# Walking the edges of two attention hops in batches of four steps

## Chip, cores and metric

The kernel runs on one core of one Trainium2 chip. The metric is the device time of one execution in microseconds (us). The kernel before takes 5588.73 us, the median of 3 runs (5587.19 to 5595.54).

## What is computed

A chain of four graph layers on 3125 nodes of 64 features and 100,000 edges (src, dst, a type of 32), each followed by a residual and a layer norm: a GIN layer, an attention layer with two hops, a GAT layer with a GRU gate, and four Chebyshev convolutions. The change is in the second layer, whose one hop is

```python
def _agg(entity_emb, relation_emb, W, head, tail, edge_type):
    a_input = jnp.concatenate([entity_emb[head], entity_emb[tail]], axis=-1)
    e = jnp.sum(a_input @ W * relation_emb[edge_type], axis=-1)
    e = jax.nn.leaky_relu(e, LEAKY_SLOPE)
    m = jax.ops.segment_max(e, head, num_segments=n)
    ex = jnp.exp(e - m[head])
    denom = jax.ops.segment_sum(ex, head, num_segments=n)
    alpha = ex / denom[head]
    return jax.ops.segment_sum(entity_emb[tail] * alpha[:, None], head, num_segments=n) + entity_emb
```

head is src and tail is dst. Per edge: a score, a maximum over all edges of the same head, and a sum weighted by the exponential of the gap to that maximum.

## The kernel before

The edges are sorted by head. 128 edges make a tile (782 of them, NT), four tiles a group (196, NG), 128 nodes a block (25, NB). A walk of BSTEPS = 196 + 25 - 1 = 220 steps goes through pairs (group, block): each step handles the four tiles of one group against one block of heads, and then either the group or the block advances. Which pair a step has is known only at run time; it is in `S.walk` and is loaded into registers with `load_row`, eight steps at a time. The walk is done once per hop, by `hop_edges`, fully unrolled.

In a step, five engines work in a pipeline with lags written out by hand in `lagged(...)`; each engine executes its stages in that order, and each stage waits on semaphores for its inputs and for buffers to come free:

- GpSimd (`on_pool`) fetches a row of 97 numbers of `dram_table` for each edge of the group (the features of the tail, a one, and its 32 scores by type), with one indirect DMA for each tile, into `ring`, which holds RG = 40 groups. It runs ahead as far as the ring allows (L969: it waits for the sum of step g - 40 + 24) and with at most 8 groups not landed.
- VectorE makes `hot` (L1102, edge against head, 0 where the edge's head is that lane) and `typed` (L1101). TensorE turns `hot` (L995), ScalarE copies the turned one to `hot_t` and counts in hop 0 (L1037). TensorE adds the tails' scores and the heads' scores, looked up by `hot_t`, in a bank (L1013, L1017).
- VectorE picks the type and sums (L1109, L1120, L1131), ScalarE spreads the score to `reach` [edge, head] with a far value where the edge isn't of that head (L1046, four instructions a step). VectorE takes the maximum over the four tiles (L1115, L1126), folds it with a running maximum kept for each block and lane, `most` (L1139, L1147); TensorE turns it (L1007), VectorE reduces it to the largest per head (L1078). ScalarE makes the factor `fade` by which older sums shrink, and keeps `held` (L1058, L1060).
- TensorE spreads the largest to all rows (L1001), VectorE subtracts (L1082), ScalarE takes the exponential (L1063), TensorE sums the rows of the ring by those weights (L983), VectorE adds the sum to the accumulator (L1092).

During the layer the first HELD = 6 of 25 blocks of the arena `adjacency` stay, and the other 19 are in `dram_adjacency`; they are written out ahead of the GIN layer (L2164) and read back after the second hop (L1272), and `gat_attention` waits for them (L1346).

Of the kernel before, what the change touches and what calls it, by code (L numbers as in the profile page):

```python
# [8 lines left out]
ALU = mybir.AluOpType  # L9
# [19 lines left out]
AHEAD = 8  # L29
# [7 lines left out]
HELD = 6  # L37
RG = 40
WRING = 8
# [897 lines left out]
def hop_edges(k, carve, cst, psum, dram, S, ring, own_parts, acc, hop):  # L937
# [3 lines left out]

    W1 = D + 1
    most = carve("most", [P, NB, P], F32)
    held = carve("held_largest", [P, NB], F32)
    hot = carve("other_source", [P, 6, P, TG], BF16)
    hot_t = carve("own_source", [P, 3, TG * P], BF16)
    reach = carve("in_reach", [P, WRING, TG, P], F32)
    typed = carve("type_hot", [P, 4, TG, NREL], BF16)
    picked = carve("picked", [P, 2, TG, NREL], F32)
    raw, score = carve("raw_score", [P, 2, TG], F32), carve("score", [P, 2, TG], F32)  # L950
    pairs, lane = carve("lane_pairs", [P, 2, 2, P], F32), carve("lane", [P, 2, P], F32)
    now, fade = carve("largest_now", [P, 4], F32), carve("fade", [P, 4], F32)
    tiles = [min(TG, NT - g * TG) for g in range(NG)]
    tails = [k.sig(f"tails{r}", 16) for r in range(8)]
    step_cols, hot_made, turned, own_made = k.sig("step_columns"), k.sig("own_hot"), k.sig("own_turned"), k.sig("own_copied")
    looked, picks, raws, scored, reached = k.sig("own_looked"), k.sig("type_picked"), k.sig("raw_made"), k.sig("step_scored"), k.sig("step_reached")
    paired, laned, most_made, lane_turned = k.sig("lanes_paired"), k.sig("lane_made"), k.sig("step_most"), k.sig("lane_turned")
    largest, spread, faded, held_made = k.sig("largest_made"), k.sig("largest_spread"), k.sig("fade_made"), k.sig("largest_held")
    kept, gaps, weighed, summed, added, counts = k.sig("most_kept"), k.sig("sum_gap"), k.sig("sum_weights"), k.sig("block_summed"), k.sig("block_added"), k.sig("degree_added")
    landed = lambda g: tails[g % 8].at(sum(tiles[g % 8:g + 1:8]) - 1)  # L960
    row = lambda t, at: t[:, bass.ds(at, 1), :].rearrange("p o c -> p (o c)")
    scores, lookups, lanes, rows, sums = psum[0:2], psum[2:4], psum[4], psum[5], psum[6:8]
# [11 lines left out]

    def on_pe(pe):
        at_j, at_r = {}, {}
        for stage, i in lagged(BSTEPS, (8, 0, 6, 5, 1)):
            if stage == 0:
                pe.wait_ge(weighed.sem, weighed.at(i))
                if i >= 2:  # L980
                    pe.wait_ge(added.sem, added.at(i - 2))
# [1230 lines left out]
```

## Time and profile before

| | us |
|---|---|
| median of 3 runs | 5588.73 |
| profiled execution | 5621.36 (span 5620.0) |
| walk of hop 1, first gather to last addition | 1341.2 to 2767.6 |
| walk of hop 2 | 2819.9 to 4235.9 |

| engine | busy us | share of the span |
|---|---|---|
| TensorE matmul | 3745.6 | 67% |
| VectorE | 3241.2 | 58% |
| ScalarE | 2395.8 | 43% |
| GpSimd | 1999.8 | 36% |

No engine is busy all the time, so the shares say little. The two walks together are half of the execution, and the change touches them, a short set-up ahead of them and the transfer of `dram_adjacency` behind them. The views to read are the busy time in stretches of a walk, and the instructions of each engine in order of time within one. A wait called "remote" is one for a semaphore whose releaser the profile doesn't show as just finished; "issue" is time in which the engine waited for nothing that the profile shows.

### The profile page before, as it was taken

What the parts mean: (1) busy time and instruction counts of PE and PEld (TensorE: products, weight loads), DVE (VectorE), ACT (ScalarE), POOL (GpSimd) and SP (SyncE); (2) the same over time, 40 slices, a digit from 0 to 9 for tenths busy, and PEclk for the clock granted to TensorE, in tenths of its full rate; (3) what the DMA queues carried; (4) which work ended last, traced back from release to release, by engine and by line L of the source; (5) the groups of instructions that cost most, each with busy time, mean ns of one, the idle gap of its engine ahead of it and who ended that gap; (6) DMA issues with size and microseconds to landing.
All of it is one profiled execution on the core that took longest, in us unless ns stands there. A gap on an engine that the chain in (4) does not pass through costs nothing. (4 is left out here: it accounts for less than half of the span.)

```text
span 5620.0 us, 85456 instructions
## 1 busy us (share of the span) xinstructions
PE 3745.6 (67%) x22845; PEld 2857.0 (51%) x22846; DVE 3241.2 (58%) x10029; ACT 2395.8 (43%) x6908; POOL 1999.8 (36%) x2011
## 2 busy tenths in 40 slices
PE   3388888692076666667803776776793188778987
PEld 0144444381076666666703766666682077654443
DVE  8888888523065555556703654554574888744444
ACT  0255555431064454445602544444462755523321
POOL 5000000333716666664073466666610065401210
PEclk6699999795555555555555555555555555578997
DMA  0000000201101111111020011111102000000000
GB/s 9 6 0 0 0 0 0 113 2 27 39 7 33 33 33 33 34 33 25 5 42 21 23 34 34 33 34 33 33 7 112 0 1 1 2 9 4 4 2 12
DMA packets 72030, 122.19 MB, mean 22 GB/s; under 512 B 40834, under 2 KB 45867, under 8 KB 71147
## 3 DMA queue, kind: packets, MB, share of 16 engines
q0 software_dynamic: 50048, 77.77, 6.1%
q1 hardware_dynamic: 20972, 24.30, 1.5%
q10 hardware_dynamic: 640, 15.65, 0.7%
q8 instruction: 175, 2.87, 0.2%
q14 instruction: 195, 1.60, 0.1%
HBM read 97.94 MB, written 19.68 MB: 21 GB/s over the span
## 5 line engine op out<-in xcount | busy, mean ns | idle before, releaser
L972 POOL DMA_INDIRECT adjacency<-dram_table,sorted_dst x1564 | 1507.9, 964 | 1413.2 <-issue 398.5
L983 PE MATMUL bank<-adjacency 128*128 x3520 | 835.9, 413 | 61.7 <-issue 61.7
L1078 DVE TENSOR_REDUCE adjacency<-bank 128x1 f32<-128x128 f32 x440 | 128.2, 291 | 1212.5 <-remote 1118.3
L983 PEld LDWEIGHTS bank<-adjacency 128*128 128x128 f32 x3520 | 767.5, 320 | 95.8 <-issue 93.3
L1017 PE MATMUL bank<-adjacency 128*128 x5280 | 313.3, 191 | 558.3 <-issue 556.2
L1017 PEld LDWEIGHTS bank<-adjacency 128*128 128x128 bf16 x5280 | 286.5, 111 | 591.3 <-issue 564.6
L1046 ACT ACTIVATE adjacency<-adjacency 128x128 f32<-128x128 bf16 x1760 | 572.1, 399 | 2.5 <-DVE adjacency L1131 2.5
L1669 PE MATMUL bank<-adjacency,cheb_parts 128*128 128x512 f16 (+1 forms) x2100 | 438.8, 368 | 51.6 <-ACTq L95 31.4
L1039 ACT ACTIVATE adjacency<-bank 128x512 bf16<-128x512 f32 x220 | 129.7, 590 | 804.8 <-remote 733.0
L995 PE MATMUL bank<-ident_b,adjacency 128*128 128x128 bf16 x1760 | 271.0, 305 | 283.7 <-DVE adjacency L1102 164.4
L1465 POOL TENSOR_TENSOR gat_z<-gat_gap,adjacency 128x512 f32<-128x512 f32 (+1 forms) x175 | 241.8, 1395 | 541.5 <-ACT gat_gap L1454 540.8
L1037 ACT ACTIVATE adjacency<-bank 128x512 bf16<-128x512 f32 x220 | 129.4, 588 | 714.8 <-remote 677.0
L553 ACT ACTIVATE adjacency<-bank 128x400 f32 x590 | 296.9, 503 | 316.9 <-PE bank L525 311.3
L522 PE MATMUL bank<-cell_hot,src_hot 128*128 128x400 f16 x1180 | 319.2, 353 | 74.5 <-DVE cell_hot L460 72.0
L995 PEld LDWEIGHTS bank<-ident_b,adjacency 128*128 128x128 bf16 x1760 | 207.6, 157 | 311.4 <-DVE adjacency L1102 188.1
L1487 PE MATMUL bank<-gat_xw,gat_z 128*128 128x65 f32 x1250 | 292.2, 423 | 72.2 <-POOL gat_z L1465 65.0
L619 POOL IOTA base_room<- 128x782 int32 x1 | 0.8, 786 | 946.1 <-ACTq L95 946.1
L1669 PEld LDWEIGHTS bank<-adjacency,cheb_parts 128*128 128x128 f16 x2100 | 200.1, 101 | 265.7 <-issue 55.0
L1013 PE MATMUL bank<-adjacency,ident 128*128 x880 | 304.5, 449 | 43.9 <-issue 29.0
L460 DVE TENSOR_SCALAR cell_hot<-iota,cell_near 128x400 f16<-128x400 f16 x1180 | 325.1, 317 | 8.4 <-ACT cell_near L544 8.4
L1487 PEld LDWEIGHTS bank<-gat_xw,gat_z 128*128 128x128 f32 x1250 | 274.3, 330 | 90.8 <-POOL gat_z L1465 76.2
L1001 PE MATMUL bank<-ident,adjacency 128*128 128x128 f32 x880 | 317.3, 463 | 0.0
(447 smaller groups left out, 8049.4 us busy)
## 6 DMA issues: line engine op xcount, KB each, us to landing
adjacency<-dram_table,sorted_dst POOLq DMA_INDIRECT x1564
dram_adjacency<-adjacency ACTq DMA_DIRECT2D x1, 15200.0 KB, 38.2
adjacency<-dram_adjacency SPq DMA_DIRECT2D x1, 15200.0 KB, 40.2
dram_table<-adjacency SPq DMA_DIRECT2D x2, 1212.5 KB, 12.3
dram_nodes<-x_nodes SPq DMA_DIRECT2D x1, 800.0 KB, 3.4
x_nodes<-dram_nodes SPq DMA_DIRECT2D x1, 800.0 KB, 4.3
x_nodes<-in_x SPq DMA_DIRECT2D x1, 768.0 KB
out_nodes<-x_nodes SPq DMA_DIRECT2D x1, 768.0 KB
```

Of the source, the lines that this page charges most:

```text
L460: ins = dve.tensor_scalar(one_c[:, r, t, :], cst.iota16[:, 0:NB * WIN], cell[:, i % CELLS, t:t + 1], None, ALU.is_equal)
L522: ins = pe.matmul(psum[r][:, 0:NB * WIN], one_b[:, r, :, t], one_c[:, r, t, :], start=(t == 0), stop=False)
L553: act.activation(A4[:, :, bass.ds(at_j[i], 1), :], psum[i % RING][:, 0:NB * WIN].rearrange("b (a o w) -> b a o w", w=WIN, o=1), ACT.Copy). ...
L972: pool.indirect_dma_start(ring[:, j % (RG * TG), :], None, dram["table"], bass.IndirectOffsetOnAxis(ap=S.dst_i[:, j:j + 1], axis=0)).then_ ...
L983: ins = pe.matmul(sums[i % 2][:, 0:W1], reach[:, i % WRING, t, :], ring[:, bass.ds(at_r[i], TG), :][:, t, 0:W1], start=(t == 0), stop=(t = ...
L995: ins = pe.matmul(scores[i % 2][:, t * P:(t + 1) * P], hot[:, i % 6, :, t], cst.ident_b[:, :], start=True, stop=True)
L1001: pe.matmul(rows[:, 0:P], now[:, i % 4:i % 4 + 1].to_broadcast([P, P]), cst.ident[:, :], start=True, stop=True).then_inc(spread.sem, 1)
L1013: pe.matmul(bank[:, 0:TG * NREL], cst.ident[:, :], ring[:, bass.ds(at_r[i], TG), W1:ROW], start=True, stop=False)
L1017: ins = pe.matmul(bank[:, t * NREL:(t + 1) * NREL], hot_t[:, i % 3, t * P:(t + 1) * P], row(own_parts[:, :, m * NREL:(m + 1) * NREL], at_j ...
L1046: ins = act.activation(reach[:, i % WRING, t, :], hot[:, i % 6, :, t], ACT.Identity, scale=-FAR, bias=score[:, i % 2, t:t + 1])
L1487: ins = pe.matmul(bank(c, j)[:, 0:D + 1], z[:, r, j * P:(j + 1) * P], xw[:, a, :], start=(a == 0), stop=(a == NB - 1))
L1669: ins = pe.matmul(bank[:, 0:n * P], parts[:, a, c0:c1], A[:, a, f * P:(f + n) * P], start=(a == 0), stop=(a == NB - 1))
```

## The change

The steps are handled in batches of SB = 4: 55 batches in a hop, and every semaphore counts batches, except those of the running maximum, the accumulator and the degree, which are still done step by step.

- Each bank now holds the four steps of a batch (`lookups`, `lanes`, `rows`, `sums`, two banks each). Elementwise work of four steps becomes one instruction: `typed`, `hot`, the pick, its sum, the score, the maxima over tiles, the reduction, the subtraction and the exponential.
- `hot` is not turned any more: L995 and the evacuation L1037 go. `hot_t` is made by VectorE with one comparison per step of `src_row`, a row of the group's 512 head numbers that SyncE fetches from `dram_src_rows` to all 128 partitions, one DMA per step. A set-up writes that table (7 transposes, 7 copies, 2 DMAs). In hop 0 ScalarE reads `hot_t` once more to count.
- `most` goes: the running maximum is kept per head only (`held`), by three small VectorE instructions a step, and `fade` is one ScalarE instruction a batch.
- GpSimd waits at the start of every fourth group for the lookup of the batch before the last one and for the turned maxima of the batch before that.
- The ring has 44 groups, and HELD is 3: 22 blocks are written out and read back.
- Registers are loaded four steps at a time, by each stage that needs them.

The core of the diff (TensorE's stages are lookup, spreading of rows, sums, transposes, in that order; ScalarE's are exponential, fade, reach, columns, counts):

```diff
-HELD = 6
-RG = 40
-WRING = 8
+HELD = 3
+RG = 44
+SB = 4
     def on_pool(pool):
         for g in range(NG):
+            burst = g // SB
+            if g % SB == 0:
+                if burst >= 2:
+                    pool.wait_ge(looked.sem, looked.at(burst - 2))
+                if burst >= 3:
+                    pool.wait_ge(lane_turned.sem, lane_turned.at(burst - 3))
             if g >= 8:
                 pool.wait_ge(tails[g % 8].sem, landed(g - 8))
             if g >= RG:
-                pool.wait_ge(summed.sem, summed.at(g - RG + NB - 1))
+                pool.wait_ge(summed.sem, summed.at((g - RG + NB - 1) // SB))
...
+    def on_sp(sp):
+        for b in range(batches):
+            at_g = steps(sp, S.walk, (slice(0, 1), 0), b, TP - TG)
+            if b:
+                sp.wait_ge(own_made.sem, own_made.at(b - 1))
+            for s in range(SB):
+                flat = dram["src_rows"][bass.ds(at_g[s], TG), :].rearrange("(o t) q -> o (t q)", o=1)
+                sp.dma_start(src_row[:, s, :], flat.to_broadcast([P, TG * P])).then_inc(rows_in.sem, 16)
...
     def on_pe(pe):
-        for stage, i in lagged(BSTEPS, (8, 0, 6, 5, 1)):
+        for stage, b in lagged(batches, (0, 2, 3, 1)):
...
-                    ins = pe.matmul(scores[i % 2][:, t * P:(t + 1) * P], hot[:, i % 6, :, t], cst.ident_b[:, :], start=True, stop=True)
-                ins.then_inc(turned.sem, 1)
...
     def on_act(act):
+        for stage, b in lagged(batches, (5, 4, 3, 0, 2)):
...
-                    ins = act.activation(hot_t[:, i % 3, :], scores[i % 2][:, 0:TG * P], ACT.Copy, scale=-1.0, bias=1.0, accum_out=S.step_count[:, i:i + 1])
+                    act.activation(counted_out[:, :], hot_t[:, b % 2, s, :], ACT.Copy, accum_out=S.step_count[:, i:i + 1]).then_inc(own_counted.sem, 1)
...
     def on_dve(dve):
-        for stage, i in lagged(BSTEPS, (6, 7, 9, 0, 3, 5, 3, 5, 3, 5, 5)):
+        for stage, b in lagged(batches, (3, 5, 4, 6, 3, 1, 3, 1)):
...
+                for s in range(SB):
+                    i = b * SB + s
+                    before = held[:, bass.ds(at_j[s], 1)]
+                    if s:
+                        dve.wait_ge(largest.sem, largest.at(i - 1))
+                    dve.tensor_tensor(now[:, b % 2, s:s + 1], before, most[:, s:s + 1], ALU.max)
+                    dve.scalar_tensor_tensor(zero_gap[:, b % 2, s:s + 1], before, most[:, s:s + 1], before, ALU.max, ALU.subtract).then_inc(rise_made.sem, 1)
+                    dve.wait_ge(rise_made.sem, rise_made.at(i))
+                    dve.tensor_copy(before, now[:, b % 2, s:s + 1]).then_inc(largest.sem, 1)
...
+                for s in range(SB):
+                    ins = dve.tensor_scalar(hot_t[:, b % 2, s, :], src_row[:, s, :], cst.block_lane[:, bass.ds(at_j[s], 1)], None, ALU.is_equal)
+                ins.then_inc(own_made.sem, 1)
```

VectorE's stages, in the order of the new lags: 0 pick, sum and score (lag 3); 1 subtraction (5); 2 reduction and running maximum (4); 3 addition to the accumulator (6); 4 degree, hop 0 only (3); 5 `typed` and `hot_t` (1); 6 maxima over tiles (3); 7 `hot` (1).

## Rows read from the trace of the kernel before

**Rows 1.** Three stretches of hop 1: us, busy by engine, PEclk, DMA share, GB/s.

```profile
1341.00:1541.00 200.00, 14.48 (x116) 9.72 (x116) 13.08 (x41) 12.31 (x47) 151.38 (x160) 0.50 0.17 40
1664.00:2629.00 965.00, 665.87 (x4507) 595.31 (x4507) 495.90 (x2021) 470.81 (x1709) 600.62 (x621) 0.50 0.15 33
1600.00:1650.00 50.00, 48.14 (x386) 45.82 (x386) 42.49 (x175) 40.66 (x145) 0.00 (x0) 0.57 0.01 2
```

**Rows 2.** TensorE in order of time: start, us, line, tiles, count, idle before.

```profile
2010.42 0.63 PE L995 MATMUL bank<-ident_b,adjacency 128*128 128x128 bf16 x4
...
2012.05 0.43 PE L1017 MATMUL bank<-adjacency 128*128 x7
2013.73 0.19 PE L1017 MATMUL bank<-adjacency 128*128 x1 [1.25 <-issue]
2015.17 0.18 PE L1017 MATMUL bank<-adjacency 128*128 x1 [1.26 <-issue]
2016.61 0.26 PE L1017 MATMUL bank<-adjacency 128*128 x3 [1.26 <-issue]
```

**Rows 3.** GpSimd in order of time, around the same stall.

```profile
2013.98 0.94 POOL L972 DMA_INDIRECT adjacency<-dram_table,sorted_dst  x1 [0.30 <-issue]
2017.52 0.94 POOL L972 DMA_INDIRECT adjacency<-dram_table,sorted_dst  x1 [2.59 <-remote]
```

**Rows 4.** Waits from 2000 to 2700: us in total, times, longest.

```profile
ACT adjacency L1037 <- remote: 315.3, 51, 6.6
DVE adjacency L1078 <- remote: 276.7, 51, 5.7
...
POOL adjacency L972 <- remote: 128.1, 50, 2.7
...
DVE adjacency L1139 <- issue: 9.7, 16, 1.0
```

**Rows 5.** Start of hop 1, in order of time: a turned step, and its reader.

```profile
1353.91 0.59 PE L995 MATMUL bank<-ident_b,adjacency 128*128 128x128 bf16 x4
...
1405.93 0.60 ACT L1037 ACTIVATE adjacency<-bank 128x512 bf16<-128x512 f32 x1 [45.32 <-remote]
```

**Rows 6.** Groups of hop 1 by shape: busy us, mean ns of one, idle before.

```profile
L983 PE MATMUL bank<-adjacency 128*128 x1760 | 418.0, 414 | 0.5 <-issue 0.5
...
L1046 ACT ACTIVATE adjacency<-adjacency 128x128 f32<-128x128 bf16 x880 | 286.0, 399 | 1.2 <-DVE adjacency L1131 1.1
...
L1082 DVE TENSOR_TENSOR adjacency<-adjacency,bank 128x512 f32<-128x512 f32 x220 | 149.2, 678 | 1.7 <-PE bank L1001 1.1
...
L1063 ACT ACTIVATE adjacency<-adjacency 128x512 f32<-128x512 f32 x220 | 135.3, 615 | 1.4 <-DVE adjacency L1082 1.4
L1037 ACT ACTIVATE adjacency<-bank 128x512 bf16<-128x512 f32 x220 | 129.4, 588 | 714.8 <-remote 677.0 <-PE bank L995 37.5
...
L1102 DVE TENSOR_TENSOR adjacency<-iota_st,step_src 128x512 bf16<-128x512 bf16 x220 | 91.8, 417 | 0.0
...
L1139 DVE TENSOR_TENSOR adjacency<-adjacency 128x128 f32<-128x128 f32 x220 | 64.5, 293 | 33.6 <-issue 18.1 <-DVE adjacency L1126 0.3
```

**Rows 7.** L460: min, median and max ns of one, the nearest comparison to `hot_t`.

```profile
L460 DVE TENSOR_SCALAR cell_hot<-iota,cell_near x1180: 310/317/326, 232.7 to 1065.5; 128x400 f16<-128x400 f16 x197
```

**Rows 8.** L972: min, median and max ns of one gather.

```profile
L972 POOL DMA_INDIRECT adjacency<-dram_table,sorted_dst x1564: 938/944/1305, 1341.2 to 4096.7; - x196
```

**Rows 9.** The transfer back: KB, us to landing.

```profile
adjacency<-dram_adjacency SPq DMA_DIRECT2D x1, 15200.0 KB, 40.2
```

More of the change, by code:

```diff
@@ L28 @@
 MAGIC = 12582912.0
-AHEAD = 8
 NGA = -(-NT // TGA)
@@ L942, in hop_edges @@
     W1 = D + 1
[L943 to L951, printed above, removed]
@@ L952, in hop_edges @@
-    now, fade = carve("largest_now", [P, 4], F32), carve("fade", [P, 4], F32)
+    held, zero_gap = carve("held_largest", [P, NB], F32), carve("rise", [P, 2, SB], F32)
+    hot = carve("other_source", [P, 2, SB, P, TG], BF16)
+    hot_t = carve("own_source", [P, 2, SB, TG * P], BF16)
+    counted_out = carve("counted_out", [P, TG * P], BF16)
+    src_row = carve("source_row", [P, SB, TG * P], F16)
+    reach = carve("in_reach", [P, 3, SB, TG, P], F32)
+    typed = carve("type_hot", [P, 2, SB, TG, NREL], BF16)
@@ L956, in hop_edges @@
[L956 to L959, printed above, removed]
+    step_cols, hot_made, own_made, rows_in = k.sig("step_columns"), k.sig("other_hot"), k.sig("own_hot"), k.sig("source_rows_in", 16)
@@ new lines, in on_pe @@
+                ins.then_inc(looked.sem, 1)
+            elif stage == 1:
+                pe.wait_ge(largest.sem, largest.at(b * SB + SB - 1))
+                if b >= 2:
+                    pe.wait_ge(gaps.sem, gaps.at(b - 2))
+                for s in range(SB):
+                    ins = pe.matmul(rows[b % 2][:, s * P:(s + 1) * P], now[:, b % 2, s:s + 1].to_broadcast([P, P]), cst.ident[:, :], start=True, stop=True)
+                ins.then_inc(spread.sem, 1)
+            elif stage == 2:
+                at_r = steps(pe, S.slots, (slice(0, 1),), b, RG * TG - TG)
+                pe.wait_ge(weighed.sem, weighed.at(b))
+                if b >= 2:
+                    pe.wait_ge(added.sem, added.at((b - 2) * SB + SB - 1))
+                for s in range(SB):
+                    for t in range(TG):
+                        ins = pe.matmul(sums[b % 2][:, s * W1:(s + 1) * W1], reach[:, b % 3, s, t, :],
+                                        ring[:, bass.ds(at_r[s], TG), :][:, t, 0:W1], start=(t == 0), stop=(t == TG - 1))
+                ins.then_inc(summed.sem, 1)
+            else:
+                pe.wait_ge(laned.sem, laned.at(b))
+                if b >= 2:
+                    pe.wait_ge(most_made.sem, most_made.at(b - 2))
+                for s in range(SB):
+                    ins = pe.transpose(lanes[b % 2][:, s * P:(s + 1) * P], lane[:, b % 2, s, :], cst.ident[:, :])
+                ins.then_inc(lane_turned.sem, 1)
@@ L1158, in hop_edges @@
         tails[r].close(sum(tiles[r::8]))
-    for s in (hot_made, turned, own_made, looked, picks, raws, scored, reached, paired, laned, most_made, lane_turned, largest, spread, faded,
-              held_made, kept, gaps, weighed, summed, added) + ((step_cols, counts) if hop == 0 else ()):
+    for e in (k.act, k.pe, k.pool, k.sp):
+        e.wait_ge(rows_in.sem, rows_in.at(BSTEPS - 1))
+    for s in (hot_made, own_made, looked, typed_made, picks, raws, scored, reached, paired, laned, lane_turned, most_made, spread, faded, gaps,
+              weighed, summed) + ((step_cols,) if hop == 0 else ()):
+        s.close(batches)
+    for s in (rise_made, largest, added, rows_in) + ((own_counted, counts) if hop == 0 else ()):
         s.close(BSTEPS)
@@ L1266, in layer_attention @@
     on_dve(dve)
+    for e in (sp, act, pe, dve, k.pool):
+        e.wait_ge(rows_out.sem, rows_out.at(1))
     relation_in.close(2)
```

303 lines of the change are left out of this document (152 added, 151 removed).

## The prediction

> **What bounds the kernel now.** I read the stretches of a walk first. With GpSimd silent (1600 to 1650) a step takes 50 us / (386 / 29 matmul records a step) = 3.76 us, with TensorE busy for 48 of 50 us, VectorE for 42 and ScalarE for 41 [rows 1]: TensorE's own pace. But in the long middle of the hop, where GpSimd gathers, 965 us hold 4507 / 29 = 155 steps, or 6.2 us a step, and no engine is over 70% busy. In the first 200 us, where GpSimd issues its 160 gathers without a pause, all of TensorE's work is 116 records, four steps' worth [rows 1]. The clock is 0.50 to 0.57 of full speed in all of them, the lower of its two levels and little above, so it doesn't explain a factor.
>
> Then the order of time says how. TensorE runs at speed up to the seventh matmul of L1017 and then gives one per 1.44 us [rows 2], though nothing it needs is late. The stall ends at 2016.61; GpSimd's last gather before it began at 2013.98 and took 0.94, so the stall ends 1.7 us after that issue. GpSimd itself then waits, 2.59 us instead of the usual 0.30, for a sum that TensorE had made long before, and starts its next 8 gathers [rows 3]. This repeats 51 times in 700 us: ScalarE at L1037 and VectorE at L1078 wait about 6 us for TensorE each time, "remote" [rows 4]. The start of the hop is the same at its worst: the fourth turned step was issued at 1353.91 and read at 1405.93, 51 us later [rows 5]. So I read: after four or five gathers in a row (about 4 us), what TensorE finishes is told to the others only when GpSimd pauses, and TensorE goes on for some 20 to 30 matmuls before it stalls. Why, no row says. VectorE's and ScalarE's own signals show no such delay.
>
> The walk is thus a cycle: 8 gathers x 1.25 us (0.944 [rows 8] and 0.30 of issue) and a pause of 2.3 more give 12.5 us for two steps. A walk takes 1426 us in hop 1 and 1416 in hop 2, of which the gathers are 782 x 1.25 = 977.
>
> A page of the Trainium skill speaks against this reading. SBUF — State Buffer, section "SBUF: two separate sides", says that TensorE and ScalarE never wait on anyone's port and that DMA and compute can't slow each other. Rows 2 and 5 show TensorE's signals late exactly while gathers run, so here the trace decides; if the page's rule held all the same, the third rival below would come out.
>
> **The change, part by part, for a batch of four steps.**
>
> GpSimd: 16 gathers instead of 4 x 4, same number in all, 20.0 us. The new waits come once in 16 gathers. Behind them on its queue are only gathers; who waits for those is TensorE's lookup of the same batch.
>
> TensorE: L995 goes (4 records a step; 0.42 us from start to start), so 4 x 3.76 - 4 x 0.42 = 13.4 us of work, 100 records instead of 116. L983, the largest (414 ns, 8 records a step [rows 6]), is unchanged.
>
> VectorE: fp32 costs (678 - 293) / 384 = 1.0 ns an element by L1082 and L1139 [rows 6], with 0.15 us fixed. bf16 with both operands packed costs half: L1102 has 417 ns for 512. New: `hot` 1.2, `typed` 0.7, pick 0.7, sum 0.7, score 0.2, maxima 1.2 + 0.7, reduction 0.7, subtraction 2.3, additions 4 x 0.28 + 0.2 for their chain, the running maximum 4 x 3 small ones, some 1.9 with its own waits, and `hot_t` 4 x 0.36, by L460 (317 ns for 400) [rows 7]; together 13.3 us, 0.6 more in hop 0 for degrees, less 2 for the overlap of neighbours: 11 to 12, against 42.5 x 3.76 x 4 / 50 = 12.8 before. The bound of `hot_t` from below is a quarter of that, from above 4 x 0.68. The register loads are finer: each load of eight shows some 0.6 us of idle (16 waits, 9.7 us, L1139 [rows 4]); VectorE has now four loads in a batch instead of one, so 0 (hidden) to 1.8 us more; I take 1.5.
>
> ScalarE: reach 16 x 0.33 from start to start = 5.2 us (unchanged), exponential 0.2 + 2048 x 0.8 ns = 1.9 (4 x 0.615 before [rows 6]), fade 0.3 instead of 1.9, counting in hop 0 4 x 0.7, as L1037 before; in hop 2 nothing instead of 4 x 0.59. Between 7.4 and 11.7 us: never the bound.
>
> One batch alone, with GpSimd silent: VectorE's stage 0 (1.4), stage 1 (2.3), stage 2 (2.7), then fade and reach on ScalarE (5.5), then maxima (1.9), the transposes (1.2) and again stage 2. Stages 0 and 1 of the next batch fill the gap, so a batch is about 15 us, with loads 16.5. This equals the 15.0 of four steps before: batching as such gains nothing where GpSimd is silent.
>
> With GpSimd running, the question is how much must pass from TensorE to the others in one burst of 16 gathers. Going through the waits: an iteration of VectorE needs `looked`, `spread`, `lane_turned` and `summed` of TensorE's iteration three before it, and none of its own time. So one release per batch is enough. In the first 4 us after a release TensorE does the lookup (56 records, 3.3 us); the other 44 go partly into the 20 to 30 that it can run ahead and partly at one per 1.44 us. GpSimd's next burst needs the turned maxima of the previous one, which are told in its pause. The cycle is then 20.0 + 2.3 for the pause, and I add 0.7 for what may not fit and for `hot_t` against GpSimd: 23.0 us a batch instead of 25.
>
> The start is the larger gain. Before, 200 us for a handful of steps; now two bursts (40 us) and then the cycle. The hop: 40 + 47 x 23.0 + the end. Behind the last gather lie some 10 iterations, 7 full ones x 16.5 + 25 = 140 us (139 before). Sum 1261 us a hop, against 1426 and 1416: 320 us less in both.
>
> Set-up: 7 transposes, 7 copies and two DMAs with everybody waiting for the last: +8 us (0 to 15). Read-back: 40.2 us for 19 blocks [rows 9], exposed before, now 22: 40.2 x 3/19 = +6 us. The write-out is hidden by the GIN layer, far longer than it. The 220 DMAs of SyncE a hop (128 rows of 1 KB each) land beside a queue at 15% share [rows 1], and the next is issued a whole batch ahead: 0, at most 2 us a batch if they were late.
>
> 5621.4 - 320 + 14 = 5315 us for the profiled execution. The median lies 32.6 below the profiled one before; so 5283 us.
>
> **Rivals.**
>
> 1. The open window is too short (slower than before from a point). Bursts of 16 are twice those of 8, and rows 5 show what a long one does: 51 us for one signal. If TensorE's 100 records don't fit in 4 us + 30 records + 10 at 1.44 us, the rest is done in the pause, which grows for 47 batches in each hop: 25.5 us gives 5283 + 94 x 2.5 = 5518, and from 26.2 (a pause of 6 us) the kernel is slower; 28 us, where TensorE has only its first 5 us and does the remaining 8 in the pause, gives 5753. For it: TensorE's share of progress in bursts was 0 at the start. Against: at each cycle of 8 it did 58 records in 12.5 us, about the same rate as 100 in 23.
>
> 2. `hot_t` holds GpSimd back. Gathers take up to 1305 ns where the median is 944 [rows 8], next to VectorE's copies. If each comparison delays a gather by its whole length, 4 x 0.36 = 1.5 us a batch: 5283 + 94 x 1.5 = 5424. The Trainium skill (the same page and section) describes such a block, for a VectorE instruction in a two-port mode against descriptors that GpSimd writes; rows 8 agree in kind, with 0.2 to 0.36 us a hit.
>
> 3. The starvation goes away. If it came from something that the change removes (the transposes L995, or running 8 groups ahead), the batch is 20.3 us: 5283 - 94 x 2.7 = 5029. GpSimd is then the bound. The 200 us at the start, where little L995 ran, speak against it.
>
> 4. The rows of head numbers arrive late, or the finer waits make a batch 25 us even so: 5283 + 188 = 5471, counted with rival 1.
>
> **How the numbers follow.** Forecast (22 to 24.4 us a batch) 0.45; rival 2 0.10; rival 3 0.12; rival 1 (with 4) up to the break-even 0.20, around it 0.03, slower 0.10. The time is that of the forecast, 5283; the range 5020 to 5530 takes in rival 3, rival 2 and most of rival 1. About 0.2% is what a measurement of this kernel can tell from no change. Faster 0.87, same 0.03, slower 0.10.
>
> **What would show it.** In the profile after: walks of about 1260 us; GpSimd in bursts of 16 with one wait of 2 to 3 us between them; 22 to 24 us a batch; about 116 records of TensorE's work no longer missing in the first 200 us; 16 to 17 us a batch behind the last gather. A pause over 5 us is rival 1, gathers over 1.2 us on average rival 2, bursts without a pause rival 3. A batch over 20 us behind the last gather would show my VectorE chain wrong, and with it the sum.

## The result, and the profile of the changed kernel

The changed kernel takes 5624.34 us (median of five runs, 5614.51 to 5633.47), the kernel before, timed beside it, 5590.68 (5587.19 to 5596.52). The ratio is 1.0057, 95% interval 1.0042 to 1.0072: slower by 0.6%. The forecast was 5283 us; it is outside the range of 5020 to 5530, and of the wrong sign.

The page of the changed kernel, the lines that answer to the table ahead of the prediction and to [rows 9]:

```profile
span 5622.9 us, 74646 instructions
...
PE 3468.9 (62%) x21092; PEld 2637.5 (47%) x21093; DVE 3212.1 (57%) x7938; ACT 2113.5 (38%) x5595; POOL 2091.2 (37%) x2011
...
adjacency<-dram_adjacency SPq DMA_DIRECT2D x1, 17600.0 KB, 46.0
```

The span is 2.9 us above that of before. This hides two changes of opposite sign. I measure a hop from the start of its first gather to the end of its last addition into `acc`. Hop 1 went from 1426.5 to 1501.1 us, hop 2 from 1416.0 to 1336.1. The set-up moved the first gather from 1341.2 to 1352.5, and the transfer back takes 46.0 us instead of 40.2 [rows 9]. These four together are 11.8 us more. The stretches ahead of hop 1 and between the hops are otherwise as before, so what follows hop 2 is 9 us shorter apart from the transfer; why, no row that I read says.

Behind the last gather hop 1 takes 147 us and hop 2 138, where each took 138 before. So most of the difference is in the gathers' stretch. Here it is for both hops, GpSimd's gathers alone (stretch, its length, their busy time, clock, DMA share, GB/s):

```profile
1352.50:2706.40 1353.90, 789.53 (x782) 0.57 0.21 49
2905.80:4104.00 1198.20, 809.58 (x782) 0.53 0.24 55
```

Divided by 782/16 = 49 batches this is 27.6 us a batch in hop 1 and 24.5 in hop 2, against a forecast of 23.0. In the kernel before the stretches are 1288.6 and 1277.9 us, 26.3 and 26.1 for four steps with the start of the hop and 25.0 in the cycle alone. One batch of hop 1 in GpSimd's order of time:

```profile
2095.60 0.94 POOL L989 DMA_INDIRECT adjacency<-dram_table,sorted_dst  x1 [8.50 <-PE bank L1043]
...
2104.35 1.29 POOL L989 DMA_INDIRECT adjacency<-dram_table,sorted_dst  x1 [0.30 <-issue]
2105.95 1.56 POOL L989 DMA_INDIRECT adjacency<-dram_table,sorted_dst  x1 [0.30 <-issue]
...
2125.02 0.94 POOL L989 DMA_INDIRECT adjacency<-dram_table,sorted_dst  x1 [8.76 <-PE bank L1043]
```

I call the gathers between two pauses a burst. Here it is sixteen in 20.7 us, then a wait of 8.76 us for the turned maxima (L1043) where [rows 3] show 2.59. And the same batch cut at the same places, for all engines (length, busy time and count of TensorE, its weight loads, VectorE, ScalarE and GpSimd, then clock, DMA share, GB/s):

```profile
2095.60:2100.60 5.00, 3.74 (x50) 3.26 (x50) 3.02 (x17) 2.66 (x10) 3.78 (x4) 0.84 0.15 35
2100.60:2105.60 5.00, 0.91 (x3) 0.65 (x3) 4.24 (x12) 4.06 (x18) 4.08 (x4) 0.51 0.29 55
2105.60:2116.26 10.66, 1.60 (x6) 1.66 (x6) 1.09 (x1) 2.17 (x6) 8.22 (x9) 0.50 0.35 79
2116.26:2125.02 8.76, 7.02 (x43) 6.99 (x44) 4.45 (x5) 1.91 (x1) 0.00 (x0) 0.50 0.02 6
```

These four rows are the result. A record is one line of the profile; an fp32 matmul leaves two. Of the 102 matmul records in them TensorE gets 50 through in the first 5 us of the gathers, 3 in the next 5, 6 in the last 10.7, and 43 when GpSimd has stopped. Over the 39 bursts of hop 1 that have 16 gathers the medians are 48 in the first 5 us, 3 more up to 10 us, 58 by the burst's end and 42 in a pause of 8.4 us. In the order of time the crawl looks as in [rows 2]:

```profile
2098.14 0.94 PE L1026 MATMUL bank<-ident,adjacency 128*128 128x128 f32 x6
2099.83 0.34 PE L1026 MATMUL bank<-ident,adjacency 128*128 128x128 f32 x1 [0.75 <-issue]
...
2113.34 0.27 PE L1035 MATMUL bank<-adjacency 128*128 x1 [1.14 <-issue]
2115.42 0.27 PE L1035 MATMUL bank<-adjacency 128*128 x1 [1.82 <-issue]
2117.55 0.27 PE L1035 MATMUL bank<-adjacency 128*128 x1 [1.86 <-issue]
2118.26 5.16 PE L1035 MATMUL bank<-adjacency 128*128 x23 [0.45 <-issue]
```

That is one record per 1.4 to 2.1 us, and then 23 without a gap, from 2 us after the last gather ended. The turned maxima for which GpSimd waits (L1043) stand behind all these products in TensorE's order, so the pause lasts until the products are through. The waits of 2000 to 2600 us, which answer to [rows 4]:

```profile
DVE adjacency L1092 <- remote: 219.9, 19, 11.8
ACT adjacency L1050 <- DVE adjacency L1105: 180.1, 20, 12.4
POOL adjacency L989 <- PE bank L1043: 149.1, 19, 9.4
POOL adjacency L989 <- issue: 99.1, 315, 2.0
ACT adjacency L1079 <- remote: 93.4, 19, 7.5
```

L1092 is VectorE's pick. It waits 11.6 us for each batch's lookups (219.9 / 19), "remote", that is for TensorE.

### The profile page after: what moved, and what is told of

Its sections match the earlier page's. It is cut to its first block and busy times, and to the rows that moved or that the text cites. A ratio compares the mean times of both kernels' runs of the same rounds, so it can differ in the third digit from the quotient of the medians.

```text
span 5622.9 us, 74646 instructions
## 1 busy us (share of the span) xinstructions
PE 3468.9 (62%) x21092; PEld 2637.5 (47%) x21093; DVE 3212.1 (57%) x7938; ACT 2113.5 (38%) x5595; POOL 2091.2 (37%) x2011
## 5 line engine op out<-in xcount | busy, mean ns | idle before, releaser
L989 POOL DMA_INDIRECT adjacency<-dram_table,sorted_dst x1564 | 1599.2, 1022 | 1328.4 <-issue 533.4
L1035 PE MATMUL bank<-adjacency 128*128 x3520 | 804.9, 383 | 680.1 <-issue 678.7
L1035 PEld LDWEIGHTS bank<-adjacency 128*128 128x128 f32 x3520 | 779.5, 311 | 739.7 <-issue 739.0
L1050 ACT ACTIVATE adjacency<-adjacency 128x2048 f32<-128x2048 f32 x110 | 210.2, 1911 | 1028.4 <-DVE adjacency L1105 867.8
L1063 ACT ACTIVATE adjacency<-adjacency 128x128 f32<-128x128 bf16 x1760 | 536.9, 394 | 94.0 <-DVE adjacency L1101 94.0
L1092 DVE TENSOR_TENSOR adjacency<-bank,adjacency 128x512 f32<-128x512 f32 x110 | 75.8, 689 | 768.3 <-remote 745.7
L1017 PE MATMUL bank<-adjacency 128*128 x5280 | 267.7, 190 | 223.8 <-issue 222.7
L1017 PEld LDWEIGHTS bank<-adjacency 128*128 128x128 bf16 x5280 | 260.3, 110 | 267.3 <-issue 243.9
L1026 PE MATMUL bank<-ident,adjacency 128*128 128x128 f32 x880 | 203.9, 372 | 187.9 <-issue 106.6
L1013 PEld LDWEIGHTS bank<-adjacency,ident 128*128 128x128 f32 x880 | 219.5, 303 | 205.4 <-issue 204.2
L1105 DVE TENSOR_TENSOR adjacency<-adjacency,bank 128x2048 f32<-128x2048 f32 x110 | 251.0, 2282 | 23.0 <-remote 21.3
L1113 DVE TENSOR_REDUCE adjacency<-bank 128x4 f32<-128x512 f32 x110 | 75.8, 689 | 307.9 <-remote 231.7
```

The costliest lines, as they stand in the source:

```text
L989: pool.indirect_dma_start(ring[:, j % (RG * TG), :], None, dram["table"], bass.IndirectOffsetOnAxis(ap=S.dst_i[:, j:j + 1], axis=0)).then_ ...
L1013: pe.matmul(bank[:, s * TG * NREL:(s + 1) * TG * NREL], cst.ident[:, :], ring[:, bass.ds(at_r[s], TG), W1:ROW], start=(s == 0), stop=False)
L1017: ins = pe.matmul(bank[:, at:at + NREL], hot_t[:, b % 2, s, t * P:(t + 1) * P], row(own_parts[:, :, m * NREL:(m + 1) * NREL], at_j[s]), st ...
L1035: ins = pe.matmul(sums[b % 2][:, s * W1:(s + 1) * W1], reach[:, b % 3, s, t, :], ring[:, bass.ds(at_r[s], TG), :][:, t, 0:W1], start=(t == ...
L1063: ins = act.activation(reach[:, b % 3, s, t, :], hot[:, b % 2, s, :, t], ACT.Identity, scale=-FAR, bias=score[:, b % 2, s * TG + t:s * TG ...
L1105: dve.tensor_tensor(reach[:, b % 3], reach[:, b % 3], rows[b % 2][:, :].rearrange("p (s c) -> p s c", c=P).unsqueeze(2).to_broadcast([P, S ...
```

## The experiments

My theory was the prediction's: TensorE's matmuls and signals come late while gathers follow each other. Against it stood: the gathers themselves are slower (VectorE holds GpSimd back), the row fetches or the batch wait cost, or the lateness has another cause. The changed kernel as it stands was traced only on chips where TensorE is late (the result, `e5_after_again`, `e10_after_other_chip`); its variants without the new waits or without the row fetches were traced only on the others.

**A chip on which nothing is late.** The first four kernels ran on one chip, and there the kernel before takes 4962.71 us (13 runs, 4961.09 to 4967.34), not 5590. Each kernel of a group below ran beside the kernel before on its own chip, so only ratios within a group are compared.

`e1_before_paced` adds to the kernel before the wait alone:

```
+            if g >= 8:
+                pool.wait_ge(looked.sem, looked.at(g - 8))
```

> The kernel before with one more wait: GpSimd starts group g only when the lookup of group g - 8 is made. Theory A (TensorE's signals are late while gathers run without a pause): the start of a hop, 200 us for four steps before, becomes paced like the rest, so 36 steps that took 324 us take 36 x 6.2 = 225; the middle stays at 6.2 us a step; 2 x 100 us less, about 5400 us. Theory B (the first steps of a hop are slow for another reason, or the ring's lead is needed): no gain, 5590 or more.

Measured: 4962.86 us, ratio 0.9999 (0.9990 to 1.0009). Its two stretches of hop 1, beside [rows 1]:

```profile
1341.00:1541.00 200.00, 146.61 (x1081) 128.81 (x1081) 119.75 (x484) 117.69 (x420) 151.39 (x160) 0.50 0.16 41
1664.00:2230.00 566.00, 457.75 (x3259) 406.02 (x3258) 358.82 (x1461) 346.94 (x1237) 428.88 (x450) 0.50 0.16 41
```

1081 matmul records in the first 200 us, not 116, beside the same 160 gathers. A hop takes 1095 and 1092 us; the gathers are its bound (983 us for 782, 1.257 each), and no gather waits longer than the usual 0.3 us. What I had called the property of this kernel depends on the chip. The new wait never held GpSimd here, so what it would do where TensorE is late stays open.

`e2_after_unpaced` takes GpSimd's new waits out of the changed kernel:

```
-            if g % SB == 0:
-                if burst >= 2:
-                    pool.wait_ge(looked.sem, looked.at(burst - 2))
-                if burst >= 3:
-                    pool.wait_ge(lane_turned.sem, lane_turned.at(burst - 3))
```

> The changed kernel without GpSimd's two new waits: only the ring of 44 groups holds it. Theory A: the first 44 groups (176 gathers, 220 us) run almost without progress elsewhere, and a hop is 100 us or more longer: 5800 us. If the waits are what costs (GpSimd pauses 7 to 9 us at them in hop 1), the kernel gets faster: a hop tends to 977 + 140 us, below 5300.

Measured: 5107.72 us, ratio 1.0290 (1.0273 to 1.0307). Where no matmul is late, the change without these waits costs 2.9%: a hop's gathers take 1024.5 and 1033.1 us instead of 983, its end 134 instead of 111, set-up and read-back are added. A gather's shortest, median and longest time:

```profile
L983 POOL DMA_INDIRECT adjacency<-dram_table,sorted_dst x1564: 940/944/1993, 1351.0 to 3591.5; - x196
```

The median is that of [rows 8], the longest 1993 ns instead of 1305. Whether the new waits or the length of the burst make the pauses where TensorE is late, this run can't say: it never ran on such a chip.

`e3_after_no_rows` fetches 64 bytes a step in place of 128 KB after the first batch, so that the own one-hots of all later steps are not computed from their rows:

```
-                sp.dma_start(src_row[:, s, :], flat.to_broadcast([P, TG * P])).then_inc(rows_in.sem, 16)
+                if b:
+                    sp.dma_start(src_row[0:1, s, 0:32], flat[:, 0:32]).then_inc(rows_in.sem, 16)
+                else:
+                    sp.dma_start(src_row[:, s, :], flat.to_broadcast([P, TG * P])).then_inc(rows_in.sem, 16)
```

> The changed kernel with SyncE's row fetches cut from 128 x 1 KB to one piece of 64 bytes a step after the first batch, so that the comparison for hot_t reads old rows and the output is wrong from there; every instruction and wait stays. If those transfers (DMA share 0.21 against 0.15 before) are what makes TensorE late, the pauses of GpSimd fall from 7 to 9 us to 2 to 3 in hop 1 and the kernel takes about 5350 us. Theory A (gathers alone do it): less than 1% changes, 5570 to 5630.

Measured: 5119.06 us, ratio 1.0313 (1.0292 to 1.0333). The nearest run with the fetches is `e2_after_unpaced`, which also leaves out GpSimd's new waits; but here no gather waits longer than 0.3 us at them, and the kernel is not faster. So the row fetches cost nothing there.

`m1_probe` computes nothing of the reference. TensorE repeats a round of 4 fp32 and 12 short bf16 matmuls, VectorE reads the bank, and beside it runs one kind of transfer: none, 56 gathers by GpSimd, 56 plain transfers by GpSimd, 56 by SyncE.

> A kernel of stages instead of the reference's computation. In stages 1 to 4 TensorE does 30 rounds of 4 fp32 and 12 short bf16 matmuls with a signal to VectorE and back, two rounds ahead, beside (1) nothing, (2) 56 indirect gathers of 128 rows of 388 bytes, (3) 56 plain transfers of the same shape from GpSimd's queue, (4) the same from SyncE's. Stages 5 to 7: ScalarE and VectorE hand a tile to and fro 60 times, beside nothing, the gathers, SyncE's transfers. Theory A, if the gathers themselves delay TensorE: stage 1 about 75 us; stage 2 TensorE slows after some 4 us to one record per 1.4 to 2.8 us until the gathers end at 70 us, so it ends at 120 us or later; stages 5 and 6 equal. If any transfer does it, stages 3, 4 slow too; if it needs the descriptors that GpSimd writes, stage 3 is slow and 4 is not.

Measured: 458.38 us, 2.11 us a round in every stage of TensorE.

**A chip on which they are late.** The next four ran where the kernel before takes 5611.31 us.

> The kernel before, unchanged, for its trace on this chip. Theory A (the late matmuls belong to the kernel): waits of GpSimd of 2.6 us every eight gathers, hop 1426 us. Theory B (they come with the chip): none, hop 1095 us, 5.03 us a step.

Measured: 5613.89 us, hops of 1422 and 1416 us with 79 waits of GpSimd each, as in [rows 3]: theory A in the numbers, but theory B in the cause, since the kernel before takes 4962.71 us on the other chip and `e1_before_paced`, whose added wait never held it, has no such waits there.

> The changed kernel once more, unchanged, so that the kernels of this call have it beside them on their own chip. If the long waits of GpSimd belong to the kernel (theory A), a hop takes 1336 to 1501 us here as in its first profile and the kernel before takes 5590. If they come from the chip on which the pair was timed (theory B), the kernel before takes about 4963 here, the changed one some 150 us more (5110): 782 gathers per hop at 1.31 us instead of 1.25 (+45 a hop), an end of a hop of 134 instead of 111 us (+23 a hop), set-up +12, read-back +6.

Measured: 5711.94 us (5674.34 to 5725.82), ratio 1.0188 (1.0168 to 1.0208); hops of 1528 and 1363 us in the profile. The changed kernel differs more from one such chip to the next than the kernel before (5711.94 against 5624.34; 5611.31 against 5590.68).

The same probe as `m1_probe`:

> The probe of single loads beside a round of matmuls once more, on this chip. It took 458.4 us with 2.11 us a round of TensorE in the stages with gathers and without. If the kernel before takes 4963 us on this chip the same is expected; if it takes 5590 us, the round should be longer in the stages with gathers (over 2.5 us), and not in those without.

Measured: 510.89 us. The 52 us are all in the stage with gathers: TensorE made only two rounds between 97 and 164 us and the rest when the gathers were done. Plain transfers by GpSimd or SyncE, with as many bytes, held nothing back, and the stages of VectorE and ScalarE took the same on both chips. So it is gathers on GpSimd against TensorE, with no part of this kernel needed.

`e4_split_maxima` makes the three long VectorE instructions that a gather can meet in four pieces each:

```
-                dve.tensor_tensor(pairs[:, :, :, :], reach[:, b % 3, :, 0:2, :], reach[:, b % 3, :, 2:4, :], ALU.max).then_inc(paired.sem, 1)
+                for s in range(SB):
+                    ins = dve.tensor_tensor(pairs[:, s], reach[:, b % 3, s, 0:2, :], reach[:, b % 3, s, 2:4, :], ALU.max)
+                ins.then_inc(paired.sem, 1)
...
```

> The changed kernel with the three long VectorE instructions of a batch (the two maxima of the scores and the one-hot of the slots, 1.2 us each) made as four short ones each, the same bytes in all. Theory 1 (a gather that starts while one of these runs waits until it ends): with pieces of about 0.35 us a gather can wait for a fourth as long; the mean gather falls from 1.02 to about 0.96 us, the gathers' stretch of a hop from 1025 to about 985 us, the kernel is 60 to 90 us faster than the changed one. Theory 2 (the gathers are slow by VectorE's total work on these tiles, or by the row fetches): mean gather stays at 1.02, and nine more instructions a batch at 0.07 us leave the time the same or up to 30 us longer.

Measured: 5839.63 us, ratio 1.0411 (1.0393 to 1.0429). A miss, and the most useful one. The gathers did what theory 1 says: their mean fell from 1007 and 1036 ns to 968 and 977. But the kernel was 128 us slower than the changed one beside it. I repeated both (`e10_after_other_chip`, `e11_split_other_chip`) where the kernel before takes 5591.99 us.

> The changed kernel, unchanged. Where the kernel before takes 4963 us: GpSimd's new waits cost nothing beyond the 5105 to 5108 us of the same kernel without them (its gathers are its bound, 1.31 us each, and no bank is late): 5100 to 5125, ratio 1.029. If they do cost, over 5150. Where the kernel before takes 5590 us or more: 5624 to 5730.

> The changed kernel with the long VectorE instructions in four pieces. Where TensorE's matmuls come late it was slower (5840 against 5712) although its mean gather fell from 1.02 to 0.97 us. Where they don't (before at 4963 us), theory 1 (a gather waits for the VectorE instruction that it starts under) says that the gathers' stretch of a hop falls from 1025 and 1036 to 985 to 1000 us and the kernel takes 5020 to 5060 us against 5110; if the gathers' delay is no bound there, the same time or more.

Measured: 5623.77 us, ratio 1.0055 (1.0044 to 1.0067), and 5807.99 us, ratio 1.0386 (1.0366 to 1.0406). The gathers' stretches of the two, hop 1 and hop 2, first the changed kernel and then the split version:

```profile
1349.10:2697.70 1348.60, 786.29 (x782) 0.57 0.21 49
2895.50:4088.20 1192.70, 807.76 (x782) 0.52 0.23 55
```

```profile
1348.90:2731.40 1382.50, 757.27 (x782) 0.57 0.20 48
2933.10:4277.80 1344.70, 762.56 (x782) 0.57 0.21 49
```

The gathers are busy 29 and 45 us less, and the second stretch is 1345 us long instead of 1193. GpSimd's pauses grew from 161 to 358 us in that hop, and a burst of 16 there lets 59 matmul records through (median) instead of 85. Quicker gathers, longer pauses: I read from it that on such a chip the slow gathers are a relief for TensorE. The split also gives VectorE nine more instructions a batch, and no run takes the two apart. How a gather gets slow can be seen in hop 2 of the changed kernel, VectorE above and GpSimd below:

```profile
3521.23 1.23 DVE L1166 TENSOR_TENSOR adjacency<-adjacency 128x1024 f32<-128x1024 f32 x1 [0.78 <-ACT adjacency L1063]
3522.49 0.69 DVE L1170 TENSOR_TENSOR adjacency<-adjacency 128x512 f32<-128x512 f32 x1
3523.10 1.22 DVE L1176 TENSOR_TENSOR adjacency<-iota_st,step_src 128x2048 bf16<-128x2048 bf16 x1
...
3525.77 2.28 DVE L1105 TENSOR_TENSOR adjacency<-adjacency,bank 128x2048 f32<-128x2048 f32 x1
```

```profile
3513.76 0.94 POOL L989 DMA_INDIRECT adjacency<-dram_table,sorted_dst  x1 [2.42 <-remote]
...
3521.63 1.65 POOL L989 DMA_INDIRECT adjacency<-dram_table,sorted_dst  x1 [0.30 <-issue]
3523.58 1.56 POOL L989 DMA_INDIRECT adjacency<-dram_table,sorted_dst  x1 [0.30 <-issue]
3525.44 0.95 POOL L989 DMA_INDIRECT adjacency<-dram_table,sorted_dst  x1 [0.30 <-issue]
3526.69 0.95 POOL L989 DMA_INDIRECT adjacency<-dram_table,sorted_dst  x1 [0.30 <-issue]
```

The gather of 3521.63 starts under L1166 and ends 0.1 us behind L1170, 0.7 us over the usual 0.94. The next starts 0.7 us before the end of L1176 and takes 0.6 us more than usual. The two under L1105, the longest of the four instructions, take their usual time; it has one input in a bank, where the others have both in SBUF. Over both hops 73 gathers that overlap L1176 and no other VectorE instruction over 0.15 us take 1.55 us in the mean, 83 that overlap L1105 alone 0.945. TensorE meanwhile, in the same burst:

```profile
3518.27 6.93 PE L1035 MATMUL bank<-adjacency 128*128 x32
3525.00 1.06 PE L1043 MATMUL bank<-ident,adjacency 128*128 128x128 f32 x4
```

32 records without a stall, from 4.5 to 11.4 us after the burst began, where hop 1 has its crawl. Sorted by their longest gather, the bursts of 16 of both hops fall apart: 33 with 1.5 to 1.6 us let 58 records through and end in a pause of 7.8 us on average; 35 with 1.6 to 1.8 let 83 through and end in 3.3 us. But this is nearly a sorting by hop: 30 of the 33 are of hop 1, 27 of the 35 of hop 2, and the 8 of the 35 that are of hop 1 let only 67 through. So it is a correlation that doesn't explain the difference between the hops, which otherwise differ in the work of `hop == 0` alone.

**What lets TensorE through.** `m3_probe_pauses` runs nine stages with 56 gathers (none in the first): without a pause; with a GpSimd memset of 0.98 us after each gather; with one of 1.82 us after eight; continuous again with rounds of 4 matmuls, of 32, and with eight more small VectorE instructions a round; with 64 and with 32 rows a gather.

> Nine stages of 30 rounds of TensorE (4 fp32 matmuls and 12 short bf16 ones, a signal and VectorE's read of the bank), with 56 gathers beside them in all but the first. On a chip that shows no late matmuls every stage's round takes 2.11 us. Where they are late: continuous gathers stop the rounds until the gathers end, as in the first probe (two rounds in 60 us). Theory N: a pause of 1 us after each gather, or of 2 us after eight, lets most rounds through; 64 or 32 rows a gather do the same if descriptors are the cause and nothing if the number of gathers is; rounds of 4 matmuls get further than rounds of 32 (a queue of instructions that drains slowly), in proportion to their instructions; eight more small VectorE instructions a round change nothing if only TensorE's path is slow, and stop the rounds sooner if all engines share it.

Measured first where the kernel before takes 4963.50 us: 771.15 us, 2.11 us a round in all stages of 16 matmuls. Its continuous stage is the first row; the eight stages on the chip of `e10_after_other_chip` follow.

> The probe of nine stages once more (30 rounds of TensorE in each, with 56 gathers in all but the first). Where the kernel before takes 4963 us every stage's round takes 2.11 us, as on the chip before. Where it takes 5590 us or more: the rounds stop under continuous gathers; if a pause is what lets them through, the stages with 1 us after each gather and 2 us after eight are 30 us or more shorter; if descriptors count, so are those of 64 and 32 rows; if TensorE's instructions drain one by one, rounds of 4 matmuls end far earlier than rounds of 32.

```profile
86.00:157.30 71.30, 62.65 (x598) 62.53 (x597) 6.73 (x30) 53.02 (x56) 1.00 0.18 40
```

```profile
86.00:157.20 71.20, 13.96 (x118) 12.65 (x117) 0.90 (x4) 52.95 (x56) 1.00 0.20 39
214.80:337.00 122.20, 62.69 (x598) 62.58 (x598) 6.74 (x30) 106.25 (x111) 1.00 0.12 23
344.60:425.20 80.60, 60.33 (x558) 59.10 (x557) 5.68 (x26) 63.82 (x63) 1.00 0.18 35
432.60:503.60 71.00, 19.38 (x86) 18.44 (x86) 2.02 (x9) 52.78 (x56) 1.00 0.20 39
543.50:614.60 71.10, 13.12 (x120) 11.17 (x119) 0.45 (x2) 52.79 (x56) 1.00 0.20 39
689.80:760.90 71.10, 14.28 (x112) 12.77 (x111) 1.40 (x36) 52.79 (x56) 1.00 0.20 39
820.70:889.30 68.60, 12.03 (x99) 10.88 (x98) 0.67 (x3) 50.35 (x56) 1.00 0.13 20
952.80:1019.20 66.40, 12.09 (x96) 10.88 (x96) 0.67 (x3) 48.30 (x56) 1.00 0.07 11
```

Each row is one stage from its first to its last gather: TensorE's busy time and matmuls first, GpSimd's last. Measured in all: 1091.15 us. Under 56 gathers in a row TensorE gets 86 to 120 records through, whatever the rounds hold, whatever VectorE does, and whether a gather has 128, 64 or 32 rows (118, 99, 96). So it goes with the gathers in a row, hardly with their descriptors or bytes; "descriptors are the cause" fell here. With 1 us between gathers 598 of the stage's 600 get through. With one pause of 1.8 us after eight, 558 do. The clock is 1.00 in every row, so it has no part in it. The order of time of the same stage shows the kind:

```profile
93.27 0.52 PE L178 MATMUL bank<-mv,w 128*128 128x32 bf16 x12
96.20 1.97 PE L176 MATMUL bank<-mv,w 128*128 128x65 f32 x8 [2.41 <-issue]
...
111.03 1.97 PE L176 MATMUL bank<-mv,w 128*128 128x65 f32 x8 [11.35 <-issue]
...
119.82 0.19 PE L178 MATMUL bank<-mv,w 128*128 128x32 bf16 x1 [2.61 <-issue]
122.62 0.18 PE L178 MATMUL bank<-mv,w 128*128 128x32 bf16 x1 [2.62 <-issue]
...
162.82 1.97 PE L176 MATMUL bank<-mv,w 128*128 128x65 f32 x8 [31.61 <-DVE low L181]
```

The gathers begin at 86.0. The first 8 us pass without a gap. Then TensorE gets one more round through, stands still for 11.35 us, does eight records without a gap, crawls, and from 131 on waits for VectorE, whose read of the bank is late too. The rounds go on 5 us behind the last gather. So it is not one steady rate. Late loading of code isn't what the trace shows: the one 16 KB piece on queue q8 that falls under these gathers took 0.97 us, and the five of the same stage on the other chip 0.96 in the median.

**Shorter pauses.** `m5_probe_short_pauses` varies the pause, `e12_before_short_pause` and `e13_after_short_pause` put one behind each gather of the two kernels:

```
                                         bass.IndirectOffsetOnAxis(ap=S.dst_i[:, j:j + 1], axis=0)).then_inc(tails[g % 8].sem, 16)
+                k.G(pool.memset(pause[:, :], 0.0))
```

> Eight stages of 56 gathers beside 30 rounds of TensorE, with GpSimd memsets as pauses: none; after each gather one of 1, 64 or 128 columns (about 0.1, 0.2, 0.25 us); after two 256, after four 512, after eight 1024, after sixteen 2048 columns (1 to 2 us). Where the kernel before takes 4963 us every round takes 2.11 us. Where it takes 5590: 116 matmuls get through continuous gathers and all of them with 1 us after each. Theory R (a rate: TensorE gets through what the gathers leave free, in proportion to the pauses) expects the rounds to fall steadily from 4.3 to 2.1 us with the share of pause; theory B (a backlog, emptied in any pause) expects even 0.2 us after each gather to give under 2.5 us a round, and eight gathers with 1 us to be as good as that; sixteen with 2 us are worse than eight with 1 us.

> The kernel before with a memset of 64 columns on GpSimd behind each gather, about 0.15 to 0.2 us. Where the kernel before takes 4963 us it costs 782 x 0.15 to 0.2 = 117 to 156 us a hop: 5200 to 5275. Where it takes 5590 us: if short pauses let TensorE's backlog go (theory B), GpSimd's eight gathers take 11.2 us instead of 10.0 and its 2.6 us wait for the open window goes: 782 x 1.40 = 1095 + an end of 138 = 1233 a hop instead of 1426 and 1416, 5215 to 5300 us in all. If the pauses only add (theory R, or TensorE is limited per cycle), 5590 or more.

> The changed kernel with the same pause. Where the kernel before takes 4963 us: 5107 + 2 x 782 x 0.15 = 5340 to 5400. Where it takes 5590 us, theory B: the waits of 7 and 3.4 us a batch shrink; a batch is 16 x 1.45 = 23.2 us, a hop 49 x 23.2 + 140 = 1277 instead of 1496 and 1325, so 5350 to 5420 us against 5624. Theory R: the batch stays at 25 to 28 us, 5550 to 5700.

They met a chip on which nothing is late (before 4974.73 us), so they answer only the price: 770.52 us for the probe, 5203.73 (ratio 1.0465, 1.0444 to 1.0485) and 5341.28 (1.0741, 1.0720 to 1.0762). A gather then takes 1.41 us from start to start, a hop of the kernel before 1213 us instead of 1095. Whether it brings 5591 us down to 5215 to 5300 on the other kind of chip, as expected, wasn't tried there and is open.

**Repeats.** `e7_before_paced_again`, `e8_after_unpaced_again` and `e9_after_no_rows_again` repeated the first three on another chip, which has no late matmuls either: 4962.66, 5105.22 and 5116.40 us beside 4963.50, the same ratios to 0.0005. What they were to show on a chip where TensorE is late stays open with them: the wait alone, the change without its waits, and the change without the row fetches were never timed there.

## Why the prediction was wrong, point by point

**The reading of the bound was right.** While gathers follow each other TensorE stalls, its signals come late, and a pause releases both. The probe shows it with nothing else in the kernel. What I couldn't know is that it is a matter of the chip: two of the five chips of the experiments had it (kernel before at 5592 and 5611 us), and by its time (5591) the one of the result; three had none (4963 to 4975). Each group of runs had a chip of its own, so whether it belongs to the chip or to something that held at that time, the runs don't say. The Trainium skill says under SBUF — State Buffer, section "SBUF: two separate sides", that TensorE never waits on anyone's port and that DMA and compute can't slow each other. The probe agrees on three chips (2.11 us a round with gathers and without) and disagrees on the others (118 records where 598 fit); there the measurement decides. Its rows don't say whether a port has a part in it.

**The step that failed** is rival 1's "against": "at each cycle of 8 it did 58 records in 12.5 us, about the same rate as 100 in 23". I took for a rate what is an allowance. A burst lets some 50 records of TensorE through and then almost nothing: 51 of the 58 in a burst of 8 (median), so that 7 were left for the pause and 2.6 us were enough; again 58 in a burst of 16, where 100 were wanted, so that 42 were left. In the four rows 24 of the 43 left are L1035 products, one per 0.22 us (5.16 / 23), and the turned maxima stand behind them. What the allowance counts isn't known: TensorE runs on for 7.4 us in the burst around [rows 2], 4 us in the one above, 8 us and 78 records in the probe. And that the burst's length makes the pause is read from these counts; no run of the kernel on such a chip changed the length alone. The sum had 2.3 + 0.7 for the pause; it measured 341.2 / 49 = 7.0 in hop 1 and 164.3 / 49 = 3.4 in hop 2. The same text had the right figure: "28 us, where TensorE has only its first 5 us and does the remaining 8 in the pause", with a chance of 0.10. Hop 1 is this case (27.6). The rows of before could have told: [rows 1] hold 116 records in 200 us of gathers without a pause, which is this allowance and a crawl. The 10 matmuls at 1.44 us that I counted for the rest of a burst were there (9 in the four rows). The 20 to 30 that TensorE runs ahead were not: I had put them on top of the lookup's 56, and they are part of the 50. The reading of [rows 2] that they came from was also off in a detail: the stall ends 1.7 us behind the end of the last gather (2013.98 + 0.94), not behind its issue.

**The batch's 16 gathers** were put at 20.0 us and took 20.7 and 21.3 (medians). Rival 2's mechanism is true in kind: 789.5 and 809.6 us of gathers where 754.1 were before. `hot_t` has little of it; 143 of the 145 gathers over 1.4 us stand beside the maxima and `hot` (L1166, L1170, L1176), which I had priced as VectorE's work and not as GpSimd's delay. The same page and section says that a VectorE instruction with two SBUF inputs holds the port that it shares with GpSimd for its whole length, against a GpSimd operation that reads SBUF; splitting them took hop 2's mean gather from 1033 to 976 ns (`e10_after_other_chip`, `e11_split_other_chip`), and the gathers under L1105, with one SBUF input, weren't slower, which agrees. On a chip without late matmuls this costs some 45 us a hop and is the larger part of the 2.9%. On the others the version with quicker gathers was the slower one, so there their time isn't what is lost.

**Hop 2's gain** of 80 us is what is left of the forecast's 155, and hop 1's loss of 75 replaces it. I had given both the same cycle. Why TensorE gets so much more through in hop 2 isn't settled.

**The start** was right: the first pause comes after 40.7 us, and the first 200 us hold 620 matmul records instead of 116. It was worth little by itself, since the cycles behind it got longer.

**Behind the last gather**: forecast 140, measured 147.2 and 137.9; a batch takes 15.3 and 14.8 us there, about the 15 named and below the 16.5 counted.

**VectorE's and ScalarE's pieces** hit: L1105 2.28 us (2.3), L1176 1.22 (1.2), the four of `hot_t` 1.27 (1.44), the exponential 1.91 (1.9). The parts that the prediction lists for VectorE add up to 13.1 us and not 13.3; nothing hangs on it.

**Set-up** +11.3 us (8), read-back +5.8 (6). The row fetches at 0: they weren't late (rival 4) in the trace of the changed kernel itself, where VectorE's L1160 waited for them 3 times in both hops together, 9.6 us in all. That their traffic costs nothing is shown on a chip without late matmuls and not tried on one with them.

**The profiled time**: the forecast took it to lie 32.6 us above the median, as in the kernel before. The profiled execution of the changed kernel takes what its median is (5624.35 and 5624.34). This is 33 of the 341 us missed; 315 are the two hops, the rest is small.

Rival 3 fell: the pauses of GpSimd stayed, though the transposes L995 were gone. The limit of 8 groups not landed is still in the changed kernel; the probe has neither and shows the stall.

## What to carry to other kernels

When an engine stalls beside bursts of another, count what it gets through per burst and per pause before the burst's length is changed: an allowance per burst looks like a rate as long as the burst stays the same. A long instruction on VectorE with both inputs in SBUF is also a delay of the gathers that GpSimd issues under it, so cost it twice. And a time from one chip can hold a bound that other chips don't have: the change costs 0.6% to 1.9% on one kind and, without its new waits, 2.9% on the other, for different reasons.

## What the hardware showed

- The kernel before takes 4963, 4964 and 4975 us on three chips and 5591 to 5611 on others; the timed executions on each lie within 0.2%.
- On the latter, indirect gathers in a row on GpSimd (1.25 us from start to start) let TensorE run for 4 to 8 us and then give it one matmul record per 1.4 to 2.8 us, with stops of 11 to 20 us in the probe; VectorE hears of its results late too. Plain transfers by GpSimd and SyncE don't do it, and VectorE with ScalarE isn't touched.
- About as many records get through for gathers of 32 rows as for 128 (96 against 118 in 56 gathers). A pause of 1 us behind each gather removes it (598 of 600), one of 1.8 us behind eight nearly so (558).
- A gather of 0.94 us takes up to 1.99 us beside VectorE instructions of 0.7 to 1.2 us with both inputs in SBUF, and 0.945 beside one of 2.28 us with one input in a bank.
- What differs between the chips, and why a gather can hold TensorE's instructions back, no run here says.
